# The gather of a graph attention layer: visits of 64 destination nodes with paired weights, halves emptied by ScalarE, and 440 written-out row fetches

## What is computed

```python
xp = (x @ W).reshape(N, H, C)                 # N = 3125, H = 4 heads, C = 256
a_src, a_dst = einsum(xp, att_src), einsum(xp, att_dst)
e = leaky_relu(a_src[src] + a_dst[dst], 0.2)
m = segment_max(e, dst);  ee = exp(e - m[dst]);  z = segment_sum(ee, dst)
msgs = xp[src] * (ee / z[dst])[:, :, None]
out = relu(segment_sum(msgs, dst).reshape(N, H * C) + bias)
# later: x + out, layer norm, top 2 of 8 experts, two expert matmuls with a gelu, x + result
```

## Time and profile before

| | |
|---|---|
| runs, median (lowest to highest) | 2160.82 us (2158.42 to 2164.39), 3 runs |
| profiled execution, span | 2296.1 us; no other time of that execution is given |
| TensorE busy, mean granted clock | 1959.2 us (85%), 0.919 |
| VectorE, ScalarE, GpSimd busy | 1470.6, 1137.3, 768.2 us |
| gather stage, first fetch to last emptying | 552.5 to 1303.4 us of the span |
| DMA moved | 490.15 MB, of it 334.62 MB on GpSimd's queue |

### The profile page before, as it was taken

How to read it: one execution, slowest core, us unless ns; L and a number is a source line. 1 busy time by engine, 2 the same in 40 slices (tenths; PEclk the granted TensorE clock), 3 DMA queues, 4 the chain that set the end, 5 groups by cost and what they waited for, 6 DMA issues and landing times. The chain is left out here.

```text
span 2296.1 us, 53233 instructions
## 1 busy us (share of the span) xinstructions
PE 1959.2 (85%) x14846; PEld 1318.7 (57%) x14847; DVE 1470.6 (64%) x4341; ACT 1137.3 (50%) x2499; POOL 768.2 (33%) x943
## 2 busy tenths in 40 slices
PE   6999977667878888888888589983899999999997
PEld 4666545645766667777667455652454445555553
DVE  7988859987666666666666699867543443443333
ACT  4444421113666666676666566654543443443332
POOL 1020000022555555555555232321233333333332
PEclk9999976568999999999999889995899999999999
DMA  7444544403988888888888677746646556644542
GB/s 272 134 143 136 172 131 172 186 0 114 312 281 291 286 299 287 294 296 287 287 298 294 235 249 240 228 142 234 233 169 249 212 167 239 221 160 171 176 162 80
DMA packets 135664, 490.15 MB, mean 213 GB/s; under 512 B 16900, under 2 KB 17108, under 8 KB 133410
## 3 DMA queue, kind: packets, MB, share of 16 engines
q0 software_dynamic: 95568, 334.62, 43.5%
q1 hardware_dynamic: 31954, 125.15, 15.1%
q10 hardware_dynamic: 8064, 29.36, 3.7%
HBM read 419.17 MB, written 81.17 MB: 218 GB/s over the span
## 5 line engine op out<-in xcount | busy, mean ns | idle before, releaser
L1130 PE MATMUL main_ps<-rows,O 128*128 128x256 f16 x4992 | 619.2, 283 | 125.7 <-DVE acc L1066 66.3
L1113 ACT ACTIVATE O<-O,pk 128x128 f16<-128x128 f16 x1664 | 502.9, 387 | 246.1 <-DVE O L1083 203.5
L1130 PEld LDWEIGHTS main_ps<-rows,O 128*128 128x128 f16 x4992 | 480.9, 102 | 217.9 <-issue 72.8
L1052 POOL DMA_INDIRECT rows<-projected,idx x416 | 395.5, 951 | 325.2 <-PE small_ps L1135 202.9
L1087 DVE TENSOR_SCALAR O<-O,pk 128x128 f16<-128x128 f16 x1664 | 314.6, 273 | 15.0 <-issue 0.2
L1837 PE MATMUL x_h<-w_p,gram 128*128 x1344 | 307.1, 386 | 18.4 <-ACT gram L1787 7.6
L1852 PE MATMUL x_o<-w_p,gram 128*128 x1344 | 308.0, 379 | 1.4 <-ACT gram L1806 1.4
L1886 PE MATMUL pj_ps<-gram,xsT 128*125 128x512 f16 x1200 | 271.1, 385 | 8.8 <-ACT xsT L402 5.5
L1837 PEld LDWEIGHTS x_h<-w_p,gram 128*128 128x128 f16 x1344 | 131.6, 99 | 171.6 <-issue 31.5
L1886 PEld LDWEIGHTS pj_ps<-gram,xsT 128*125 128x125 f16 x1200 | 163.2, 139 | 104.7 <-ACT xsT L402 8.6
L1083 DVE TENSOR_SCALAR O<-iota,pk 128x128 f16<-128x128 f16 x416 | 109.4, 263 | 164.9 <-PE small_ps L1135 124.1
(11 more groups left out here) (346 smaller groups left out, 2538.9 us busy)
## 6 DMA issues: line engine op xcount, KB each, us to landing
w_f<-in_L_ffn_W_dram SPq DMA_DIRECT2D x14, 2048.0 KB
b_t<-in_L_ffn_b_dram ACTq DMA_DIRECT2D x56, 512.0 KB
projected_f<-xp_f POOLq DMA_DIRECT2D x25, 500.0 KB, 3.7
projected<-xp POOLq DMA_DIRECT2D x25, 500.0 KB, 4.6
out_dram<-n_x SPq DMA_DIRECT2D x25, 500.0 KB
x_after_gnn_normed<-PK POOLq DMA_DIRECT2D x25, 500.0 KB, 9.1
xt<-in_x_dram SPq DMA_DIRECT2D x24, 512.0 KB, 3.3
n_own<-projected_f SPq DMA_DIRECT2D x24, 512.0 KB, 13.0
```

The source lines that it names most:

```text
L1052: pool.indirect_dma_start(out=rows[:, 4 * p + k, :, :].rearrange("k n d -> k (n d)"), out_offset=None, in_=xp_d[:, :], in_offset=bass.Indi ...
L1113: ins = act.activation(O[:, k, 1 + HEADS + h, :], O[:, k, 0, :], ACT.Copy, scale=pk[:, p, k, w:w + 1])
L1130: pe.matmul(main_ps[:, h * C:(h + 1) * C], O[:, k, 1 + HEADS * a + h, :], rows[:, 4 * p + k, b, h * C:(h + 1) * C], start=first and h % 2 ...
```

## The change

**The visit.** The destination nodes are cut into 50 halves (64 and 61 nodes) in place of 25 blocks. A tile is visited once from each half that it touches: 391 + 49 = 440 visits, 110 groups of four. `O` has 64 columns for each weight in place of 128, in the order high of head 0, low of head 0, high of head 1 and so on. The pair of one head fills 128 columns, and one matmul multiplies both with a part of the rows: two passes a head, eight matmuls in place of twelve. The high half of the sum then stands in 64 partitions of `main_ps` and the low half in the other 64.

**The one-hots.** One VectorE instruction makes all nine columns groups of a visit (compare and multiply, 576 elements a partition) in place of five on VectorE and four on ScalarE; `O` has eight buffers in place of four.

**The emptying.** `main_ps` and `small_ps` are doubled. ScalarE copies one half to `acc` and the other to `other_half`, then the sums; VectorE adds `other_half` to `acc` some visits later. TensorE waits at the first visit of a half only for the emptying of the half before the last.

**The fetches.** The loop on GpSimd is written out: 440 indirect DMAs, each with its index column straight from `srcT`, waiting for one constant of `ms_done`. The copy to `idx` and the waits for it and for the rows are gone.

**Ahead of the gather.** 49 counts in place of 24 (five a block in blocks 2 to 11), `visits` two blocks later and a little longer, the numbers turned in blocks 15 to 19, five larger `high_one_hots` in blocks 20 to 24 in place of eight in 17 to 24, ten chunks of 44 visits in place of eight of 52, and a copy of the node terms by half (`by_sub`).

```diff
-VISITS = TILES + BLOCKS
+SUB = 64
+SUBS = 2 * BLOCKS
+VISITS = TILES + SUBS - 1
-CHUNK = VISITS // 8
+CHUNKS = 10
+CHUNK = VISITS // CHUNKS
...
-            PER = 3
+            PER = 5
...
-                        if 2 <= i < 10:
-                            for b in range(PER * (i - 2) + 1, PER * (i - 1) + 1):
+                        if 2 <= i < 12:
+                            for b in range(PER * (i - 2) + 1, min(PER * (i - 1) + 1, SUBS)):
...
-            O = sbuf(c, "O", [P, 4, 1 + 2 * HEADS, P], F16)
+            O = sbuf(c, "O", [P, 8, 1 + 2 * HEADS, SUB], F16)
-            main_ps = psum(c, "main_ps", [P, D])
-            small_ps = psum(c, "small_ps", [P, 512])
+            other = sbuf(c, "other_half", [P, D])
+            main_ps = psum(c, "main_ps", [P, 2, D])
+            small_ps = psum(c, "small_ps", [P, 2, 512])
...
-                    steps(pool, GROUPS, body)
+                    for v in range(VISITS):
+                        if v >= 8:
+                            pool.wait_ge(s_done, v - 7)
+                        pool.indirect_dma_start(
+                            out=rows[:, v % 8, :, :].rearrange("k n d -> k (n d)"), out_offset=None, in_=xp_d[:, :],
+                            in_offset=bass.IndirectOffsetOnAxis(ap=srcT[:, v:v + 1], axis=0)).then_inc(s_row[v % 8], 16)
...
+                    def add(n, sub, odd):
+
+                        wait_apart(dve, s_met, s_drained, n)
+                        own = HALVES[odd]
+                        a = acc[:, sub // 2] if isinstance(sub, int) else acc[:, bass.ds((sub >> 1).with_bounds(min_val=0, max_val=BLOCKS - 1), 1)].squeeze(1)
+                        dve.tensor_tensor(a[own], a[own], other[own, :], ALU.add).then_inc(s_added, 1)
...
+                            dve.scalar_tensor_tensor(
+                                O[:, 4 * p + k, :, :], iota16[:, 0:SUB].unsqueeze(1).broadcast_to([P, 1 + 2 * HEADS, SUB]), pk[:, p, k, 0:1],
+                                pk16[:, p, k, 1:2 + 2 * HEADS].unsqueeze(2).broadcast_to([P, 1 + 2 * HEADS, SUB]),
+                                ALU.is_equal, ALU.mult).then_inc(s_oh, 1)
...
+                    act.nop().then_inc(s_drained, 1)
+                    for s in range(SUBS):
+
+                        own, off = HALVES[s % 2], HALVES[1 - s % 2]
+                        wait_apart(act, s_met, s_done, act.value_load(ends_i[:, s:s + 1], min_val=1, max_val=VISITS))
+                        if s >= 2:
+                            act.wait_ge(s_added, s - 1)
+                        act.activation(acc[own, s // 2, :], main_ps[own, s % 2, :], ACT.Copy)
+                        act.activation(other[own, :], main_ps[off, s % 2, :], ACT.Copy)
+                        act.activation(sacc[own, s // 2, :], small_ps[HALVES[1], s % 2, 0:2 * SUMS], ACT.Copy).then_inc(s_drained, 1)
...
                         for h in range(HEADS):
-                            if first and h % 2 == 0 and not early(v, 1):
-                                pe.wait_ge(s_seen, 3 * v - 2 + h // 2)
-                            for a, b in ((0, 0), (0, 1), (1, 0)):
-
-                                pe.matmul(main_ps[:, h * C:(h + 1) * C], O[:, k, 1 + HEADS * a + h, :],
-                                          rows[:, 4 * p + k, b, h * C:(h + 1) * C],
-                                          start=first and h % 2 == 0 and a == b, stop=True, skip_group_check=True)
+                            cols = slice(h * C, (h + 1) * C)
+                            for b in range(2):
+                                pe.matmul(main_ps[:, odd, cols], O[:, 4 * p + k, 2 * h:2 * h + 2, :].rearrange("k n c -> k (n c)"),
+                                          rows[:, 4 * p + k, b, cols],
+                                          start=first and h % 2 == 0 and b == 0, stop=True, skip_group_check=True)
```

More of the change, by code:

```diff
@@ L127, in wait_apart, with first_of, group_word, sub @@
     eng.wait_ge(sem, value)
+def first_of(sub):
+    return ROWS * (sub // 2) + SUB * (sub % 2)
 def visit_word(eng, words, n, g):
-    w = eng.value_load(words[:, n, g:g + 1] if isinstance(g, int) else words[:, n, bass.ds(g, 1)])
-    def block(u):
-        return ((w >> (BITS * u)) & ((1 << BITS) - 1)).with_bounds(min_val=0, max_val=BLOCKS - 1)
+    return eng.value_load(words[:, n, g:g + 1] if isinstance(g, int) else words[:, n, bass.ds(g, 1)], min_val=0, max_val=(SUBS << BITS) - 1)
+def group_word(eng, words, n, g):
+    w = visit_word(eng, words, n, g)
     def flag(u):
-        return (w >> (4 * BITS + u)) & 1
-    return block, flag
+        return (w >> u) & 1
+    def sub(u, flags):
+        b = w >> BITS
+        for t in flags:
+            b = b + flag(t)
+        return b
+    return flag, sub
 class Wider:
@@ L767, in load @@
                             sp.dma_start(t[p], d[CHUNK * i:CHUNK * (i + 1), :].partition_broadcast(P)).then_inc(s_row[p], 16)
-                    for i in range(1, 8):
+                    for i in range(1, CHUNKS):
                         load(i, i % 2)
@@ L810, in _ @@
                     link(dve.tensor_scalar(pen[:, :, :], pen[:, :, :], -BIG, None, ALU.mult))
-                    for i in range(7):
+                    for i in range(CHUNKS - 1):
                         body(i, i // 2, i % 2)
@@ L856, in body @@
                             at_n = slice(4 * n, 4 * n + 4) if isinstance(n, int) else bass.ds(4 * n, 4)
-                            _, block_of = nc.values_load_multi_w_load_instructions(
-                                blocks_i[:, at_n], engines=[mybir.EngineType.PE], min_val=0, max_val=BLOCKS - 1,
-                                skip_runtime_bounds_check_because="the table counts the borders at or below a visit, of which there are BLOCKS - 1")
+                            _, sub_of = nc.values_load_multi_w_load_instructions(
+                                subs_i[:, at_n], engines=[mybir.EngineType.PE], min_val=0, max_val=SUBS - 1,
+                                skip_runtime_bounds_check_because="the table counts the borders at or below a visit, of which there are SUBS - 1")
                             if not early(n, 2):
@@ L1059, in _ @@
                 @block.vector
                 def _(dve):
-                    def take(b):
-                        for n in range(2):
-                            half = slice(n * 512, (n + 1) * 512)
-                            a = acc[:, b, half] if isinstance(b, int) else acc[:, bass.ds(b, 1), half].squeeze(1)
-                            dve.tensor_copy(a, main_ps[0:ROWS, half]).then_inc(s_seen, 1)
-                        dve.tensor_copy(at(sacc, b), small_ps[0:ROWS, 0:2 * SUMS]).then_inc(s_seen, 1)
+                    def add(n, sub, odd):
[3 more added lines that the diff above has]
+                        dve.tensor_tensor(a[own], a[own], other[own, :], ALU.add).then_inc(s_added, 1)
@@ new lines, in add_ended @@
+                    def add_ended(g):
+                        ends, sub_of = group_word(dve, words, 1, g)
+                        with dve.If(ends(0) + ends(1) + ends(2) + ends(3) > 0):
+                            for u in range(4):
+                                with dve.If(ends(u) == 1):
+                                    sub = sub_of(u, range(u)).with_bounds(min_val=0, max_val=SUBS - 1)
+                                    with dve.If((sub & 1) == 1):
+                                        add(sub + 2, sub, 1)
+                                    with dve.Else():
+                                        add(sub + 2, sub, 0)
@@ L1143, in body @@
                                 continue
+                            sub = sub_of(k, range(1, k + 1)).with_bounds(min_val=0, max_val=SUBS - 1)
                             with pe.If(first_at(k) == 1):
-                                products(i, j, p, k, True)
+                                wait_apart(pe, s_met, s_drained, sub)
+                                with pe.If((sub & 1) == 1):
+                                    products(i, j, p, k, True, 1)
+                                with pe.Else():
+                                    products(i, j, p, k, True, 0)
```

258 lines of the change are left out of this document (122 added, 136 removed).

## The result

The changed kernel takes **2251.2 us** (median; 2250.16 to 2252.01 in 4 runs) against 2161.23 of before on the same chip: ratio **1.042**, 95% interval 1.0403 to 1.0437. It is 4.2% slower; the prediction of 2080 us (2030 to 2165) was wrong, in sign too.

A forecast was written before the change was run, and what follows sets the result against it. It took TensorE with its stops to bound the gather before, and transfers after: -110 + 2.5 + 9 + 11 + 1 = -86.5 us on a span of 2296.1, scaled by 0.941 to -81 on the runs: 2080 us, range 2030 to 2165.

The forecast's parts named there:

- TensorE with its stops sets the pace: Gather of the kernel before: 750 us, TensorE busy for 624; 416 visits at 1.35 us make 562, borders and slow clock 188.
- +2.5: After the last visit: two copies and an addition in line, about 2.1 + 1.7 us, where two copies stood at 1.4.
- +9: Projection, blocks 2 to 11: two more counts a block make VectorE late for the next transposes, 9 us.
- +11: Edge terms: six more groups, 6.8 us, more one-hot builds, 2.4, and larger visit tables, 1.7, on VectorE.
- +1: Behind the last block: four short copies of node terms by half, 1 us.
- TensorE: 9 matmuls in place of 13, 0.93 us a visit: New gather: 1.35 x 9/13 at full clock, 440 visits in 411 us, 0.5 us a visit to spare under the transfers.
- GpSimd: 1.25 us a fetch: New gather: written-out fetches follow one another in 1.25 us, 0.3 of it issue; 440 take 550 us.
- DMA: 363 GB/s, 1.445 us a visit: New gather: transfers bound it at 636 us, stage 640 against 750; bounds 390 and 324 GB/s; sign: TensorE waits for rows.
- rival of 306 GB/s: Gather: transfers give no more than now, 754 us, so 2190 us in the runs, slower than before; chance 0.14.
- VectorE: 0.7 us: New gather: the one-hot instruction of 576 elements takes 0.7 us; with copies and additions 1.15 us a visit, 506 us.
- VectorE as the bound: Gather: at two cycles an element the one-hot takes 1.3 us, a visit 1.75, 770 us, 2206 in all; chance 0.03.
- The clock: Gather: rival that TensorE stays at half clock, 1.81 us a visit, 796 us, 2230 in all; chance 0.03.

## Why the prediction was wrong

**"TensorE with its stops sets the pace", read from a gather of 750 us.** The engine was right: half the bytes hardly shorten the gather of before (616.7 us for 622.1). The size was not: 622 us in the execution taken again and 623 by leaving it out. I saw that the profiled span was 135 us over the median and spread the difference by a factor of 0.941; it belonged to the gather almost whole. Forecast from 622 us, the same terms give 640 - 622 = +18 for the stage, and with +2.5, +9, +11 and +1 a kernel 41 us slower, about 2202. This step alone turned the sign. The other 49 of the 90 us are the pace of the new gather (680.6 us for 640) and the work ahead, both below. Why that one execution had a slow gather stays open.

**"TensorE: 9 matmuls in place of 13, 0.93 us a visit", with "0.5 us to spare".** This is the step that failed in the mechanism. I scaled the time of the products and left out what the sequencer does between them. Before, 1.35 us of products a visit covered the one branch a visit that there is, 0.53 us of sequencer work in all; after, 2.6 branches a visit and the words they read are some 0.9 us a visit that the shorter products no longer cover. Measured: 1.53 us a visit and not 0.93, of which taking the branches away gives back 0.09, where the next bound stands.

**"GpSimd: 1.25 us a fetch".** Measured 1.113 + 0.3 = 1.41. The one-hot instruction with two inputs in SBUF stretches the fetches that it meets from 0.94 to 1.13 us on the mean, the additions those that they meet to 1.34; with one input of the one-hot in PSUM a fetch takes 1.00 on the mean of all. Hidden in the changed kernel behind TensorE, and worth 63 us (2218.7 to 2155.7) once the branch is gone. The Trainium skill, page "SBUF — State Buffer", section "🔬 SBUF: two separate sides", says that the descriptors of a DMA issued from GpSimd are generated on GpSimd, which cannot write them while VectorE runs in a mode with two ports; instructions with two SBUF inputs it counts as taking the shared port only against a GpSimd instruction that reads SBUF. The traces show the effect for two SBUF inputs, 113 ns a fetch on the mean from the one-hot, and only in part: some fetches that meet a one-hot still take 0.94 us (905.36 above). That it is this port no run shows. I had not weighed it.

**"DMA: 363 GB/s, 1.445 us a visit", the bound of the forecast.** Wrong as a bound: half the bytes made no kernel here faster that was tried with them, and the fastest moved 401 GB/s over 400 us, above even my upper bound of 390. The sign that was to show it, TensorE waiting 0.3 to 0.6 us for rows in each visit, did not come: 7.8 us in all. Its rival of 306 GB/s falls too, though the kernel did become slower, as that rival had said: from another cause.

**"VectorE: 0.7 us"** for the new instruction was 0.81 (813 ns), and VectorE was never late in the changed kernel (3.4 us ahead or more). Its rival, VectorE as the bound, falls. The rule of the Trainium skill that stood beside it (page "Vector Engine (DVE) Microarchitecture Reference", section "Points that are easy to get wrong": half the throughput with two such SBUF sources) is contradicted once more: 813 ns with both inputs in SBUF and 809 with one in PSUM. **The clock** stayed at 1.00 in the window of the gather, so that rival falls.

**Ahead of the gather** the forecast was 9 + 11 + 1 = 21 us. From the profile of before taken again to the changed kernel, the first matmul of the edge terms moved from 330.68 to 343.29 us, plus 12.6 (forecast 9), and the first fetch from 550.68 to 582.62, plus 31.9 in all; the runs without the gather say 39. The mechanism in the projection was as told: VectorE at 11.28 of 12 us, TensorE no longer at 12.00 (11.76 and 11.81 above). The term was undersized by 11 to 18 us, mostly behind the projection (19.3 for 12): there 110 groups for 104 and ten chunks for eight were counted, and the scans, products and copies over the whole table only as a lump.

## What to carry to other kernels

Compare the profiled execution's span with the runs before anything is read from it; where they differ by 6%, as here, the profile does not stand for the runs, and its longest stage is suspect. When work of an engine is cut, add up what its sequencer does between the instructions (branches, register work, words read), which no busy share shows: it can become the floor. And call the transfers a bound only when half the bytes make the kernel faster, whatever the DMA share says.

## What the runs showed of the hardware

- A branch on TensorE's sequencer took 169 to 207 ns in the median of its line, a plain register operation 32 to 36, a word read from SBUF 302. They were not covered in the changed kernel, where TensorE is busy 1.1 us a visit (285 of 400 us, 262 visits).
- DMA shares of 0.95, 0.97, 0.97 and 1.02 went with 343, 353, 362 and 401 GB/s in the same kind of fetch: the packets took longer for their bytes where the rate was lower, so a share near 1 was no sign of a full queue. Half the bytes gave 0.62 at 172 GB/s.
- Two fetches of 128 rows stand 0.30 us apart at least, and one takes 0.94 us, 4 KB or 2 KB a row. A bound on the row number adds 0.03 to 0.05 us, and rows left out save none of GpSimd's time.
- A VectorE instruction that reads two tiles in SBUF lengthens GpSimd's fetches: float16 one-hot of 576 elements, 0.94 to 1.13 us on the mean of those that met it; float32 addition of 1024, to 1.34. One input in PSUM took the first to nothing (0.94) and left the instruction as fast (813 and 809 ns).
